# Graph kernel, start of the program: edge lists loaded by ScalarE's queue, x first on SyncE's, and eight transposes of x moved in place of idle ones

## The chip, the cores and the metric

The kernel runs on one core of a Trainium2 chip, in one launch. The metric is the device time of one execution in microseconds (us). A difference is told against runs of the kernel before.

## The reference, cut to what matters

Inputs are x (1024 nodes x 512 features), 32768 edges as two int32 lists `src` and `dst` (sorted by dst), and the weights of four layers. Each layer is a graph operation with a residual and a layer norm behind it:

```
edge_index = jnp.stack([src, dst])
x = _layernorm(x + L0(x, edge_index, w0, b0))   # D^-1/2 (A or A^T, plus I) D^-1/2 @ (x @ w0) + b0
x = _layernorm(x + L1(x, edge_index, ...))      # three graph convolutions, degrees by segment_sum over dst
x = _layernorm(x + L2(x, edge_index, ...))      # attention over the edges' mask
x = _layernorm(x + L3(x, edge_index, ...))      # relu(conv), conv
```

All layers need the same 1024 x 1024 matrix of edge counts. L0 also needs x @ w0.

## The kernel before, in words

Every engine has its own program, written out by hand in the order in which it runs; semaphores join them. No planner is used. What follows is the start, up to the end of the histogram loop, and what the change touches.

**Loads.** SyncE (SP) issues the DMAs one after the other (lines 382 to 396): dst and src into `edge_rows` (64 partitions x 512 each, 128 KB each), the low half of x into `xs` (1 MB), four rows of w0 (256 KB each), the high half of x, wq and wk (1 MB each), small bias rows, w1. The edges' loads count up `edges_in`, the halves of x `x_in[0]` and `x_in[1]`.

**From edges to keys.** VectorE zeroes five blocks of `count` (L1168), waits for both edge lists, and takes the low 7 bits and the rest of src (`bits`, L1170 and L1171), then the smallest and largest dst of each group and span (`group_lim`), the relative dst (`key_rows`) and diagonal matrices of the limits (`group_dia`). ScalarE converts the bits (L1000, L1002). TensorE transposes the three rows of keys (L615, which waits for `act_rows_set` and `rows_set`), ScalarE copies the turned keys (`edge_key`, L1004), VectorE adds them up (`keyed`) and casts them (`lo16`, L1192). The limits reach all partitions by one product of ones with `group_dia` into bank 0 (L620, "the limits' product"), which VectorE copies to `group_row` (L1195) and reduces to the number of rounds. Then VectorE enters its loop with the conversion of the keys (`key16`, L1252).

**The histogram loop.** The edges form 64 groups of 512. For each, VectorE writes one-hots (`lo_near` L1207, `hot_key` L1213), ScalarE the other half of them (distances L986, `lo_far` L993), TensorE multiplies them into one of four slots of PSUM (L626), and VectorE adds the two spans at the group's place in `count` (L1229). Four slots let TensorE run ahead of VectorE by that much. VectorE makes the one-hots of three groups before its first add, and reads the places of four groups at a time into registers (`places_at`, L1221).

**Pieces.** Between the histogram's matmuls TensorE works off a list of other units, cut into four pieces each: transposes of x (L548), of wq, wk (L552) and w1, the products x @ w0 (L587) and products of weights (L560 and on). `ORDER` is the list; `pieces[g]` gives the pieces that go behind group g, shared out by fixed weights (`TURNED` = 200 for a transpose, 1024 for a piece of a product; `SHARE` = 1280 per group), and `pieces[-1]`, sized by `EARLY`, those that go ahead of the first group: pieces 0 to 21, which are 16 transposes of the low half of x (units 0 to 3), two pieces of x @ w0 and four transposes of the high half. Unit n of these writes bank 4 + n % 4; ScalarE copies each finished unit out of PSUM (`copy_unit`) in its own order, the first four behind the first two groups' distances.

**Idle turns.** `idle_turns(n)` issues n transposes of the identity into bank 7, which nothing reads (L603). There are 16 at the start, 6 ahead of the third row of keys, 8 ahead of the limits' product, and 4 ahead of the pieces.

**ScalarE's start.** Its program begins with a copy of one column of `ones` into `esum` (L998), which waits for `const_set`, then the conversions of the bits. Its one table load bears the line of that copy.

Of the kernel before, what the change touches and what calls it, by code (L numbers as in the profile page):

```python
# [40 lines left out]
BODY = 16  # L41
HALF = 4
ZEROED = 5


def gnn_kernel(nc, x, src, dst, w0, b0, w1, b1, w2, b2, w3, b3, wq, bq, wk, bk, wv, bv, v1, c1, v2, c2, out):
# [5 lines left out]
    GE = CPG * P  # L52
# [7 lines left out]
    with ExitStack() as ctx:  # L60
# [9 lines left out]
        def at(name, start, shape, dt):  # L70
            return nc.alloc_sbuf_tensor_at(name, shape, dt, offset=start)
# [7 lines left out]
        def sem(name):  # L79
            return ctx.enter_context(nc.semaphore(name))  # L80
# [48 lines left out]
        edge_rows = at("edge_rows", r3 + 2 * W, [G, 2, GE], I32)  # L129
# [70 lines left out]
        edges_in = sem("edges_in")  # L200
# [71 lines left out]
        UNITS += [("bw", 0, 0)] + each("w12") + each("wf") + [("g", 0, 0)]  # L272
        NU = len(UNITS)
        upto = {kind: n + 1 for n, (kind, _, _) in enumerate(UNITS)}

        ORDER = []
        for n, (kind, _, _) in enumerate(UNITS):
            if kind in ("tb", "bw"):
                ORDER += [(m, k) for k in range(4) for m in (n, n + 1)]
            elif kind == "xw":  # L280
                turns = [(m, k) for m in (n - 2, n - 1) for k in range(4)]
                if n == 6:
                    ORDER += [(n, 0), (n, 1)] + turns[:6] + [(n, 2)] + turns[6:] + [(n, 3)]
                else:
                    for k in range(4):
                        ORDER += turns[2 * k:2 * k + 2] + [(n, k)]
            elif UNITS[n - 1][0] not in ("tb", "bw") and not any(u[0] == "xw" for u in UNITS[n + 1:n + 3]):
                ORDER += [(n, k) for k in range(4)]
# [6 lines left out]
        def ended(m):  # L295

            return sum(k == 3 for _, k in ORDER[:m])

        pieces = {}
        n, credit = 0, EARLY  # L300
        for g in range(-1, G - 1):
            m = n
# [73 lines left out]
        def wview(w):  # L376
            return w.rearrange("(c p) n -> p c n", p=P)

        @block.sync
        def _(sp):  # L380

            sp.dma_start(edge_rows[:, 0, :], dst.rearrange("(g e) -> g e", e=GE)).then_inc(edges_in, 16)
            sp.dma_start(edge_rows[:, 1, :], src.rearrange("(g e) -> g e", e=GE)).then_inc(edges_in, 16)
            for h in range(2):
                sp.dma_start(xs[:, HALF * h:HALF * (h + 1), :],
                             x[h * D:(h + 1) * D, :].rearrange("(b p) d -> p b d", p=P)).then_inc(x_in[h], 16)
                if h == 0:
                    for k in range(FB):
                        sp.dma_start(w0_sb[:, k, :], w0[k * P:(k + 1) * P, :]).then_inc(w0_in[k], 16)
            sp.dma_start(wq_sb[:], wview(wq)).then_inc(w_in["q"], 16)  # L390
            sp.dma_start(wk_sb[:], wview(wk)).then_inc(w_in["k"], 16)
            for n, b in enumerate((bq, bk, b1, b2)):
                sp.dma_start(brow[n * FB:(n + 1) * FB, :], b.rearrange("(c p) -> c p", p=P)).then_inc(cols_in, 16)
            for t, b in ((bias0, b0), (bias3, b3), (biasv, bv), (biasc1, c1)):
                sp.dma_start(t[:], b.partition_broadcast(P)).then_inc(rows_in, 16)
            sp.dma_start(w1_sb[:], wview(w1)).then_inc(w_in["1"], 16)
            sp.wait_ge(unit_done, upto["wqT"])
            sp.dma_start(w2_sb[:], wview(w2)).then_inc(w_in["2"], 16)
            sp.wait_ge(unit_done, upto["wkT"])
            sp.dma_start(w3_sb[:], wview(w3)).then_inc(w_in["3"], 16)  # L400
            sp.dma_start(wv_sb[:], wview(wv)).then_inc(w_in["v"], 16)
            sp.wait_ge(unit_out, NU)
            sp.dma_start(fold_rows[:, :], grow[:]).then_inc(fold_kept, 16)
            sp.wait_ge(fold_kept, 16)
            for n, t in enumerate((fold1, fold2)):
                sp.dma_start(t[:], fold_rows[n, :].partition_broadcast(P)).then_inc(fold_in, 16)
            sp.wait_ge(row_out, 1)
            sp.dma_start(degrees_kept[:], deg_row[0:1, :]).then_inc(deg_kept, 16)
            sp.wait_ge(deg_kept, 16)
            sp.dma_start(degs[:, 1, :], degrees_kept[0, :].rearrange("(j p) -> p j", p=P),  # L410
                         allow_slow_non_contiguous=True).then_inc(deg_in, 16)
            sp.wait_ge(part_done, len(PARTS))
            sp.dma_start(v1_sb[:], wview(v1)).then_inc(w_in["v1"], 16)
            sp.dma_start(v2_sb[:], wview(v2)).then_inc(w_in["v2"], 16)
            sp.dma_start(biasc2[:], c2.partition_broadcast(P)).then_inc(rows_in, 16)
            for j in range(NB - 1):
                sp.wait_ge(normed, 3 * NB + j + 1)
                sp.dma_start(out[j * P:(j + 1) * P, :], xs[:, j, :]).then_inc(stored, 16)
            for n, cols in enumerate((low_cols, high_cols)):
                sp.wait_ge(normed, 4 * NB + n)  # L420
                sp.dma_start(out[N - P:N, cols], xs[:, NB - 1, cols]).then_inc(stored, 16)
            sp.wait_ge(stored, 16 * (NB + 1))

        @block.gpsimd
        def _(pool):
# [23 lines left out]
            pool.wait_ge(rows_set, 2)  # L449
            nc.gpsimd.memset(count[:, ZEROED:NB, :].bitcast(F32), 0.0).then_inc(const_set, 1)  # L450
            pool.wait_ge(unit_out, upto["bT"])
# [81 lines left out]
        def _(pe):  # L533
# [66 lines left out]
            def idle_turns(count_):  # L600

                for n in range(count_):
                    pe.transpose(bank[:, HALF + 3, 0:P], ident[:], ident[:])  # L603
# [3 lines left out]
            for n in range(3):  # L607
# [7 lines left out]
                    mm = pe.transpose(bank[:, 2 + n // 2, at_col:at_col + G],  # L615
                                      key_rows[:, n, c * P:(c + 1) * P], ident[0:G, 0:G])
                mm.then_inc(rows_turned, 1)
            idle_turns(8)
            pe.wait_ge(rows_set, 2)
            pe.matmul(bank[:, 0, 0:2 * SPANS * G], ones[0:G, :], group_dia[:].rearrange("g a b -> g (a b)"),  # L620
                      start=True, stop=True).then_inc(rows_turned, 1)
# [5 lines left out]
                                 start=c % PAIR == 0, stop=c % PAIR == PAIR - 1)  # L627


            idle_turns(4)  # L630
            for m in range(*pieces[-1]):
                piece(m)
            for g in range(G):
                pe.wait_ge(win_added, max(2, g + 3 - SLOTS))
# [319 lines left out]
        def _(act):  # L954
# [39 lines left out]
                                     scale=-1.0, bias=ones[:, 0:1]).then_inc(act_hot_set, 1)  # L994


            act.wait_ge(const_set, 1)
            nc.scalar.copy(esum[:, 0, 0:1], ones[:, 0:1])  # L998
            act.wait_ge(bits_set, 1)
# [157 lines left out]
        def _(dve):  # L1157
# [3 lines left out]
            def then(ins):  # L1161

                chain[0] += 1
                ins.then_inc(dve_set, 1)
                dve.wait_ge(dve_set, chain[0])


            then(V.memset(count[:, 0:ZEROED, :].bitcast(F32), 0.0))  # L1168
            dve.wait_ge(edges_in, 32)
# [436 lines left out]
```

## Time and profile before

| | us |
|---|---|
| median of 3 runs | 567.65 (567.15 to 568.31) |
| the profiled execution's own time | 567.68 |
| its span, from the first to the last instruction | 565.9 |
| TensorE busy | 554.7 (98%) |
| VectorE busy | 332.0 (59%) |
| ScalarE busy | 169.5 (30%) |
| GpSimd busy | 128.2 (23%) |

The profiled execution's time is 1.8 us longer than its span, and times within the profile are counted from the span's start. Engines: PE is TensorE's matmuls, PEld its weight loads, DVE VectorE, ACT ScalarE, POOL GpSimd, SPq the issuing queue of SyncE; a name with q is an engine's sequencer. The granted clock of TensorE was at 90% or more of full speed in all 40 slices of the span.

### The profile page before, as it was taken

How to read it: one execution, taken by the hardware profiler on the slowest of the kernel's cores; microseconds unless marked ns; L12 is line 12 of the kernel's file. 1: busy time of each engine (PE TensorE's matmuls, PEld its weight loads, DVE VectorE, ACT ScalarE, POOL GpSimd, SP SyncE). 2: the span in 40 equal slices, each digit the busy share in tenths (PEclk: the TensorE clock that was granted, in tenths of full speed). 3: DMA queues.
4: the chain of work that ended last, by engine and by line, in shares of the span. 5: the costliest groups of instructions: out<-in, count | busy, mean ns of one | idle time of the engine just before them, and what ended most of it. 6: DMA issues, size and time to landing. Idle time of an engine off the chain costs nothing.

```text
span 565.9 us, 6587 instructions
## 1 busy us (share of the span) xinstructions
PE 554.7 (98%) x2179; PEld 346.5 (61%) x2179; DVE 332.0 (59%) x753; ACT 169.5 (30%) x364; POOL 128.2 (23%) x129
## 2 busy tenths in 40 slices
PE   8999999999999999999999999999999999999995
PEld 6655656445788744888865674544454686468643
DVE  7989898847687034225585984956374700540165
ACT  5998687455012222011040000321123103210200
POOL 3000000027234401203226630560410340000022
PEclk9999999999999999999999999999999999999999
DMA  8724000001000000000000000000040000000012
GB/s 291 250 76 148 2 1 1 2 0 38 1 3 1 0 1 0 0 1 0 2 3 0 1 0 0 1 1 0 1 167 0 2 0 1 0 0 1 0 57 95
DMA packets 9434, 16.24 MB, mean 29 GB/s; under 512 B 1571, under 2 KB 1843, under 8 KB 9398
## 3 DMA queue, kind: packets, MB, share of 16 engines
q1 hardware_dynamic: 9398, 15.75, 7.9%
q8 instruction: 24, 0.39, 0.3%
q14 instruction: 12, 0.10, 0.1%
HBM read 13.64 MB, written 2.11 MB: 28 GB/s over the span
## 4 chain that ended last, share of the span: by engine, by line
PE 90%; DVE 5%; issue 2%; DVEq 2%; ACT 0%; POOL 0%; POOLq 0%
PE bank L716 16%; PE bank L698 16%; PE bank L768 14%; PE bank L886 13%; PE bank L908 10%; PE bank L882 4%; PE bank L626 3%; PE bank L591 2%; PE bank L560 2%; PE bank L595 2%; DVE count L1229 2%; PE bank L587 2%; PE bank L898 1%; DVE hot_key L1213 1%; PE bank L603 1%
## 5 line engine op out<-in xcount | busy, mean ns | idle before, releaser
L472 POOL TENSOR_TENSOR rstd<-veps,mhalf 128x1 f32<-128x1 f32 x32 | 22.7, 710 | 207.8 <-DVE veps L1303 204.9
L908 PE MATMUL bank<-vv,probt 128*128 128x512 f32 x128 | 56.1, 592 | 0.0
L768 PE MATMUL bank<-v_sb,gt 128*128 128x512 f32 (+1 forms) x136 | 55.3, 567 | 0.0
L1229 DVE TENSOR_TENSOR count<-bank,count 128x192 f32 x128 | 45.7, 357 | 11.9 <-PE bank L626 7.9
L716 PE MATMUL bank<-adj,y_hi 128*128 128x512 f32 x128 | 51.5, 402 | 0.0
L716 PE MATMUL bank<-adj,y_lo 128*128 128x512 f32 x128 | 50.3, 393 | 0.0
L1310 DVE SCALAR_TENSOR_TENSOR xs<-bank,dinv,xs 128x512 f32<-128x512 f32 x23 | 17.0, 749 | 49.8 <-PE bank L768 37.3
L986 ACT ACTIVATE apart<-col_lo,edge_key 128x128 bf16<-128x128 int16 x128 | 44.2, 397 | 0.7 <-PE bank L615 0.7
L768 PEld LDWEIGHTS bank<-v_sb,gt 128*128 128x128 f32 x136 | 25.8, 190 | 28.8 <-issue 27.7
L908 PEld LDWEIGHTS bank<-vv,probt 128*128 128x128 f32 x128 | 23.9, 190 | 27.7 <-issue 27.7
L1213 DVE TENSOR_TENSOR hot_key<-col_key,key 128x384 bf16<-128x384 int16 x128 | 39.7, 351 | 0.1
L587 PE MATMUL bank<-w_sb,x0t 128*128 128x512 f32 x64 | 33.0, 599 | 0.3 <-ACT x0t L962 0.3
L993 ACT ACTIVATE lo_far<-apart,ones 128x256 bf16<-128x256 bf16 x64 | 32.2, 503 | 0.0
L626 PEld LDWEIGHTS bank<-hot_key,lo_near 128*128 128x128 bf16 x128 | 12.3, 100 | 31.9 <-issue 23.9
L505 POOL TENSOR_SCALAR mask<-count 128x1024 bf16<-128x1024 uint16 x8 | 23.1, 2894 | 37.6 <-DVE peak L1483 29.7
L1558 DVE SCALAR_TENSOR_TENSOR hidden<-bank,dinv,biasc 128x512 f32<-128x512 f32 x8 | 6.0, 751 | 37.6 <-PE bank L768 37.6
L716 PEld LDWEIGHTS bank<-adj,y_hi 128*128 128x128 f32 x128 | 24.1, 188 | 6.3 <-issue 0.5
L716 PEld LDWEIGHTS bank<-adj,y_lo 128*128 128x128 f32 x128 | 24.1, 188 | 5.9 <-issue 0.5
L768 PE MATMUL bank<-wfold,gt 128*128 128x512 f32 x64 | 27.6, 592 | 0.0
L1406 DVE TENSOR_TENSOR score<-bank,score 128x512 f32<-128x512 f32 x28 | 18.8, 688 | 13.6 <-PE bank L886 13.6
L698 PE MATMUL bank<-ya_hi,adj 128*128 128x512 f32 x64 | 25.6, 401 | 0.0
L716 PE MATMUL bank<-adj,yb_hi 128*128 128x512 f32 x64 | 25.5, 398 | 0.0
(221 smaller groups left out, 1071.1 us busy)
## 6 DMA issues: line engine op xcount, KB each, us to landing
w_sb<-in_L_gnn_W_dram SPq DMA_DIRECT2D x3, 1024.0 KB, 5.6
xs<-in_x_dram SPq DMA_DIRECT2D x2, 1024.0 KB, 7.3
v_sb<-in_L_gnn_W_dram SPq DMA_DIRECT2D x2, 1024.0 KB, 6.8
out_dram<-xs SPq DMA_DIRECT2D x7, 256.0 KB, 2.0
w_sb<-in_L_gnn_weight_dram SPq DMA_DIRECT2D x4, 256.0 KB, 6.4
wq_sb<-in_L_gnn_Wq_dram SPq DMA_DIRECT2D x1, 1024.0 KB, 10.5
wk_sb<-in_L_gnn_Wk_dram SPq DMA_DIRECT2D x1, 1024.0 KB, 12.8
wv_sb<-in_L_gnn_Wv_dram SPq DMA_DIRECT2D x1, 1024.0 KB, 7.8
```

Source lines behind the costliest of these rows:

```text
L505: then(nc.gpsimd.tensor_scalar(mask[:, m % 2, :], count[:, TILES[m], 0:N], 1.0, None, ALU.min))
L587: mm = pe.matmul(to, x0t[:, k, rows], w0_sb[:, k, :], start=first, stop=last)
L626: return pe.matmul(bank[:, slot, span], lo, hot_key[:, slot, c // PAIR, :, c % PAIR], start=c % PAIR == 0, stop=c % PAIR == PAIR - 1)
L698: mm = pe.matmul(to, m[:, k, j * P:(j + 1) * P], y[part][:, k, :], start=k == 0 and part == 0 and m is mat, stop=k == NB - 1 and part == 1 ...
L716: mm = pe.matmul(to, y[part][:, k, f * P:(f + 1) * P], m[:, k, half], start=n == 0 and part == 0 and m is mat, stop=n == NB - 1 and part = ...
L768: mm = pe.matmul(bank[:, 0 if cols is high_cols else HALF * (s % 2) + b, cols], g(k, j), w[:, k, cols], start=k == 0, stop=k == FB - 1)
L886: mm = pe.matmul(to, a[:, k, n * P:(n + 1) * P], b[:, k, :], start=k == 0, stop=k == 1)
L908: mm = pe.matmul(bank[:, 6 + m % 2, :], probt[:, m % 2, j, :], vv[:, j, :], start=j == 0, stop=j == NB - 1)
L986: ins = nc.scalar.activation(apart[:, n, c - BY_DVE, :], col_lo[:], ACT.Abs, scale=-1.0, bias=edge_key[:, 0, bass.ds(g + c * G, 1)])
L993: nc.scalar.activation(lo_far[:, slot], apart[:, n], ACT.Relu, scale=-1.0, bias=ones[:, 0:1]).then_inc(act_hot_set, 1)
L1213: V.tensor_tensor(hot_key[:, slot, n], col_key[:], key16[:, bass.ds(g, 1), n * PAIR:(n + 1) * PAIR].to_broadcast([P, KEYS, PAIR]), ALU.is_ ...
L1229: return V.tensor_tensor(count[:, :, bass.ds(at_dst, WIN)], bank[:, slot, n * KEYS:(n + 1) * KEYS].rearrange("p (h d) -> p h d", h=NB), co ...
```

## The change

The two edge loads leave SyncE's program and stand at the start of ScalarE's, dst first, ahead of the copy to `esum`. SyncE's first DMA is the low half of x. On TensorE the 8 idle turns ahead of the limits' product are replaced by the first 8 pieces (`OPENED` = 8: units 0 and 1, transposes of the low half of x); the 4 idle turns behind the product go, and the list goes on with piece 8. `pieces` itself, and so what follows each group, is unchanged.

```
+OPENED = 8
...
         @block.sync
         def _(sp):
 
-            sp.dma_start(edge_rows[:, 0, :], dst.rearrange("(g e) -> g e", e=GE)).then_inc(edges_in, 16)
-            sp.dma_start(edge_rows[:, 1, :], src.rearrange("(g e) -> g e", e=GE)).then_inc(edges_in, 16)
             for h in range(2):
                 sp.dma_start(xs[:, HALF * h:HALF * (h + 1), :],
...
                 mm.then_inc(rows_turned, 1)
-            idle_turns(8)
+            for m in range(OPENED):
+                piece(m)
             pe.wait_ge(rows_set, 2)
             pe.matmul(bank[:, 0, 0:2 * SPANS * G], ones[0:G, :], group_dia[:].rearrange("g a b -> g (a b)"),
                       start=True, stop=True).then_inc(rows_turned, 1)
...
-            idle_turns(4)
-            for m in range(*pieces[-1]):
+            for m in range(OPENED, pieces[-1][1]):
                 piece(m)
...
+            nc.scalar.dma_start(edge_rows[:, 0, :], dst.rearrange("(g e) -> g e", e=GE)).then_inc(edges_in, 16)
+            nc.scalar.dma_start(edge_rows[:, 1, :], src.rearrange("(g e) -> g e", e=GE)).then_inc(edges_in, 16)
             act.wait_ge(const_set, 1)
             nc.scalar.copy(esum[:, 0, 0:1], ones[:, 0:1])
```

## Rows read from the trace of the kernel before

**Rows 1.** The page: the chain that ended last, shares of the span by engine.
```profile
PE 90%; DVE 5%; issue 2%; DVEq 2%; ACT 0%; POOL 0%; POOLq 0%
```
**Rows 2.** Waits in 12 to 47 us: us in total, times, longest us.
```profile
PEld bank L626 <- DVE count L1229: 4.0, 6, 1.4
...
PE bank L626 <- DVE hot_key L1213: 1.5, 3, 0.9
```
**Rows 3.** Stretches: us, busy us (x instructions) by engine, PEclk, DMA share, GB/s.
```profile
24.00:47.00 23.00, 21.50 (x122) 12.23 (x119) 20.07 (x77) 21.99 (x63) 0.20 (x1) 1.00 0.15 53
47.00:60.00 13.00, 13.00 (x68) 7.49 (x67) 11.84 (x46) 10.48 (x30) 0.00 (x0) 1.00 0.46 161
```
**Rows 4.** The chain within 12.2 to 46.8 us, shares by line.
```profile
by line: DVE count L1229 28.3%; issue 20.8%; DVE hot_key L1213 18.7%; DVEq L1221 12.4%; DVE lo_near L1207 8.4%; DVEq L1229 2.9%; DVEq L1207 2.8%; DVEq L1213 1.7%; DVE key L1252 1.5%; DVE base_at L1254 0.8%; DVEq L1236 0.6%; DVE shift L1255 
```
**Rows 5.** The chain within 0 to 50 us in order: start us, us, what.
```profile
12.19 0.53 DVE key L1252
...
46.35 0.36 DVE hot_key L1213
...
46.84 0.52 PE bank L626 x4
```
**Rows 6.** The timeline from 0: start us, us, engine line op out<-in xcount [idle before].
```profile
0.72 1.28 ACT L998 ACT_TABLE_LOAD   x1 [0.72 <-PEq L1597]
...
0.72 0.55 SPq L382 DMA_DIRECT2D edge_rows<-in_dst_dram  x1
...
1.33 0.57 SPq L383 DMA_DIRECT2D edge_rows<-in_src_dram  x1
1.34 2.24 DVE L1168 MEMSET count<- 128x2620 f32 x1 [1.20 <-PEq L1597]
...
1.96 0.58 SPq L385 DMA_DIRECT2D xs<-in_x_dram  x1
2.01 0.19 ACT L998 COPY esum<-ones 128x1 f32<-128x1 f32 x1
...
2.02 3.67 PE L603 MATMUL bank<-ident 128*128 128x128 f32 x16 [2.02 <-POOL ones L438]
...
4.45 0.42 DVE L1170 TENSOR_SCALAR bits<-edge_rows 64x512 int32<-64x512 int32 x1 [0.87 <-DMA edge_rows<-in_src_dram]
...
7.70 1.09 PE L603 MATMUL bank<-ident 128*128 128x128 f32 x8
...
8.21 1.22 DVE L1192 CAST lo<-edge_key 128x128 int16<-128x128 f32 x1
...
8.73 0.70 PE L620 MATMUL bank<-group_dia,ones 64*128 64x256 f32 x2
...
9.85 1.91 PE L548 MATMUL bank<-ident,xs 128*128 128x128 f32 x16
...
10.48 2.06 ACT L962 COPY x0t<-bank 128x512 f32<-128x512 f32 x4 [1.30 <-PE bank L548]
...
13.45 0.62 DVE L1213 TENSOR_TENSOR hot_key<-col_key,key 128x384 bf16<-128x384 int16 x2
...
14.36 0.34 PE L626 MATMUL bank<-hot_key,lo_near 128*128 128x192 bf16 x2
```
**Rows 7.** DMA issues in 1.9 to 2.0 us: KB each, us from issue to landing.
```profile
xs<-in_x_dram SPq DMA_DIRECT2D x1, 1024.0 KB, 6.2
edge_rows<-in_src_dram SPq DMA_DIRECT2D x1, 128.0 KB, 3.0
```
**Rows 8.** Stretches of 0.5 us, columns as in rows 3.
```profile
3.50:4.00 0.50, 0.50 (x5) 0.50 (x4) 0.08 (x1) 0.00 (x0) 0.50 (x1) 1.00 1.46 102
4.00:4.50 0.50, 0.50 (x4) 0.50 (x4) 0.05 (x1) 0.00 (x0) 0.20 (x3) 1.00 0.09 25
4.50:5.00 0.50, 0.50 (x4) 0.50 (x3) 0.50 (x2) 0.10 (x1) 0.00 (x0) 1.00 0.86 336
...
7.50:8.00 0.50, 0.50 (x7) 0.43 (x7) 0.50 (x4) 0.10 (x1) 0.07 (x1) 1.00 1.05 402
```

More of the change, by code:

```diff
@@ L43 @@
 ZEROED = 5
+OPENED = 8
 def gnn_kernel(nc, x, src, dst, w0, b0, w1, b1, w2, b2, w3, b3, wq, bq, wk, bk, wv, bv, v1, c1, v2, c2, out):
@@ L380, in _ @@
         def _(sp):
-            sp.dma_start(edge_rows[:, 0, :], dst.rearrange("(g e) -> g e", e=GE)).then_inc(edges_in, 16)
-            sp.dma_start(edge_rows[:, 1, :], src.rearrange("(g e) -> g e", e=GE)).then_inc(edges_in, 16)
             for h in range(2):
@@ L617, in _ @@
                 mm.then_inc(rows_turned, 1)
-            idle_turns(8)
+            for m in range(OPENED):
+                piece(m)
             pe.wait_ge(rows_set, 2)
@@ L627, in chunk @@
                                  start=c % PAIR == 0, stop=c % PAIR == PAIR - 1)
-            idle_turns(4)
-            for m in range(*pieces[-1]):
+            for m in range(OPENED, pieces[-1][1]):
                 piece(m)
@@ L994, in far_one_hots @@
                                      scale=-1.0, bias=ones[:, 0:1]).then_inc(act_hot_set, 1)
+            nc.scalar.dma_start(edge_rows[:, 0, :], dst.rearrange("(g e) -> g e", e=GE)).then_inc(edges_in, 16)
+            nc.scalar.dma_start(edge_rows[:, 1, :], src.rearrange("(g e) -> g e", e=GE)).then_inc(edges_in, 16)
             act.wait_ge(const_set, 1)
```

## The prediction

> **What bounds the kernel now.** I read the chain of waits on the page first, then what TensorE waited for, then busy time by stretch, and last the start in order of time. The chain [rows 1] is 90% TensorE: over the span as a whole, work taken off its queue is worth its price, and so is an earlier start of it. The change only touches the first 15 us, so the question is which engine sets the time there. From 12 to 47 us it isn't TensorE. In the histogram loop TensorE stands still for VectorE, 4.0 us for the adds into `count` and 1.5 us for the key one-hots [rows 2], and is busy 21.5 of 23 us between 24 and 47 us, while after 47 us it is never idle [rows 3]. The chain from 12.2 to 46.8 us [rows 4] has only VectorE, its queue and issue time in its large shares; it runs from the key conversion at 12.19 us to the one-hots at 46.35 us, and TensorE takes it over only at 46.84 us [rows 5]. (`count` is also said to wait for TensorE there, but the chain puts these places down to VectorE's own register loads, L1221.) So up to 46.8 us the end moves with the moment at which VectorE starts, and a TensorE that is early waits longer.
>
> VectorE's start hangs on the edges. dst and src are issued at 0.72 and 1.33 us; src lands 3.0 us after its issue, 4.33 us, and VectorE begins at 4.45 us [rows 6, 7]. Its zeroing of `count` ended at 1.34 + 2.24 = 3.58 us, so it waited 0.87 us for data. From 4.45 to 12.19 us it runs nearly without a break on what it has; the one place where TensorE stands close is the limits' product: it begins at 8.73 us and takes 0.70 us, ends at 9.43 us, and VectorE's cast ahead of the copy that reads it ends at 8.21 + 1.22 = 9.43 us too [rows 6].
>
> **Part 1: twelve idle turns go, eight transposes of x come ahead of the product.** Removed are 8 turns (1.09 us) and the 4 behind the product. The 16 early transposes took 1.91 us, 0.12 us each, so eight are 0.96 us in the place of 1.09 us [rows 6]: the product comes at 8.73 us or up to 0.13 us sooner. Sooner is worth nothing, since the cast ends at 9.43 us anyhow. Behind the product 8 fewer transposes (0.96 us) and 4 fewer idle turns (at 1.09/8 each, 0.55 us) remain: TensorE is 1.5 us ahead. ScalarE's four copies of x, now from 10.48 us, come forward with them, and so do the first products with w0, and the first histogram matmul, at 14.36 us now, waits for the one-hots of VectorE (first pair 13.45 to 14.07 us) [rows 6]. It gains at most 0.5 us, and VectorE takes up that result no sooner, as it makes the one-hots of three groups first. From there the head start lies in TensorE's wait, which grows from the 5.5 us of [rows 2]. The split of the pieces over the groups doesn't change (the constants that share them out are the same), so no work moves from behind 46.8 us to the stretch where TensorE is idle. Value of part 1: 0. Bounds: 0 from the chain, and 1.5 us of gain if all of it came through.
>
> The cover: these transposes need the low half of x at 7.70 us. It was issued at 1.96 us and landed 6.2 us later, 8.16 us [rows 6, 7]; now issued at 0.72 us, and by the same 6.2 us, it lands at 6.9 us, 0.8 us in time. The edges' 256 KB between its packets cost at most 0.26 MB / 336 GB/s = 0.8 us more [rows 8]. Each us later than 7.70 would delay the product and with it VectorE one for one.
>
> **Part 2: SP issues x at once.** Two issues of 0.55 and 0.57 us with their gaps leave SP's queue, so all its DMAs come 1.96 - 0.72 = 1.24 us sooner [rows 6]: both halves of x, w0, and everything behind. All of them feed TensorE's pieces in the loop, which the chain doesn't run through; value 0. The high half, too, is not later than before, and its reader is in the covered stretch.
>
> **Part 3: ScalarE issues the edges.** No queued work of ScalarE is late: its next need is the conversion behind VectorE's bits, later than 4.45 us. If its two issues cost what SP's did, dst goes out at 0.72 us and src at 1.33 us, as before. The table load of 1.28 us [rows 6] would then run from about 1.9 to 3.2 us, beside the flight of the edges. What changes is company: x's 1 MB goes out with dst instead of behind src. The trace shows what x brings. From its issue at 1.96 us it took until about 4.5 us for the DMA engines to move data at full rate; in 3.5 to 4.0 us they were more than fully busy at 102 GB/s, in 4.0 to 4.5 us 25 GB/s passed, then 336 [rows 8]. Moved by 1.24 us, that slow stretch falls on 2.3 to 3.3 us, when the edges' bytes pass now. From 3.3 us the rest passes at 336 GB/s or more, shared with x: for src alone 2 x 0.131 MB / 336 GB/s = 0.8 us, for both twice that, 1.6 us. Last bytes at 4.1 to 4.9 us, and I add 0.3 us to the semaphore (an estimate): landing at 4.4 to 5.2 us, 0.1 to 0.9 us later than 4.33. I take 0.3 us later, near the lower end, as dst is out as early as x and part of it will slip through. Bounds: earlier by 0.4 us (below); later until all of x is in, 6.9 + 0.8 = 7.7 us, 3.4 us.
>
> The Trainium skill (DMA: Bandwidth & Descriptors, section Queues, rings and completion order) says that each DMA engine takes turns between queues by whole packets, 9 to 17 descriptors typically, and that a completion is written only after every earlier write of that engine, across its queues. It speaks against this change. The rows show each load on one queue alone and can't confirm it; the sum by it is the second rival below.
>
> **Sum.** 0 + 0 + 0.3 us. The profiled execution took 567.68 us at a span of 565.9 us, and the median of the runs is 567.65 us, the same. Forecast: 567.95 us, which is no change: the three runs spread over 1.2 us, and a difference under 0.2% (1.1 us) can't be told.
>
> **Rivals.**
> 1. Slower: the table load stays ahead of the DMA issues. It began at 0.72 us, the instant at which ScalarE's block starts, though the copy whose line it bears waited until 2.01 us [rows 6]. Both a load at the head of the block and one right ahead of that copy fit. If it is at the head, dst goes out at 2.0 us and src at 2.6 us, 1.28 us late, and with x already flowing I add 0.2 us: 569.1 us. It decides as soon as the load is the first instruction. The Trainium skill (ScalarE: Activation LUTs, section Step-by-step: what each stage is for) says that the load is placed right before the activation that needs it. By that rule this rival falls. Chance 0.15.
> 2. The edges queue behind runs of x's packets, as DMA engines take turns by runs of descriptors. A run in front of src of a third to a half of x's 2.7 us or more (1.05 MB at 402 GB/s [rows 8]) costs 0.9 to 1.4 us, the bound being 3.4 us: 568.8 us, and over 569 us in its tail. For it: the DMA engines were more than fully busy once x came. Against: only 64 rows of each edge list are to go in. Chance 0.09.
> 3. The edges come sooner, on a queue of their own. VectorE could start at 3.58 instead of 4.45 us. But TensorE's first 16 idle turns end at 5.69 us [rows 6], and the row transposes stand behind them; they now end nearly as the rows come. That leaves about 0.4 us: 567.25 us. Chance 0.11.
> 4. TensorE's 1.5 us comes through after all (the chain as inferred hides a wait for its chunks): 566.2 us. For it: ScalarE and VectorE are both nearly full in 24 to 47 us, and their order could be freed by it [rows 3]. Against: [rows 2, 5]. Chance 0.05.
>
> The clock: a new pause of about 1 us may come ahead of the first histogram matmul; pauses of up to 1.4 us [rows 2] left the granted clock at 1.00 in these stretches [rows 3], so I price it at nothing.
>
> **Chances and range.** Forecast 0.60. Faster by over 0.2% (below 566.5): rival 4 and a little noise, 0.06. Slower by over 0.2% (above 568.8): rival 1 most of the time, half of rival 2 and a tail of the forecast (src over 1.1 us late), 0.20. Within: 0.74. The range is 567.0 to 569.3 us: below it lie rival 4 and the lucky side of rival 3, above it the long waits of rival 2.
>
> **What would show it.** In the changed kernel's profile: ScalarE's first DMA issue at 0.7 us with the table load behind it (rival 1: at 2.0 us); VectorE's `bits` at 4.5 to 5.2 us; the product's start no more than 4.3 us behind `bits`, as now; transposes of x from 7.7 to 8.0 us without a wait for the DMA; the first `key` conversion 7.7 us behind `bits`; TensorE's wait for VectorE in 12 to 47 us larger by 1 to 1.5 us; and the 46.84 us moved by what `bits` moved. The forecast is wrong if `bits` moves by over 1 us, or if the end moves by something other than `bits` did.

## The result, and the profile after

The changed kernel takes 573.51 us (median; 573.21 to 574.10, 5 runs) against 567.65 us, a ratio of 1.0097 with a 95% interval of 1.0077 to 1.0116: 5.9 us slower. Its profiled execution took 573.51 us at a span of 571.7 us.

The timeline of the changed kernel from its start; the columns are those of rows 6, and ACTq is ScalarE's issuing queue.

```profile
0.72 0.44 SPq L384 DMA_DIRECT2D xs<-in_x_dram  x1
0.72 0.56 ACTq L996 DMA_DIRECT2D edge_rows<-in_dst_dram  x1
...
1.32 0.61 ACTq L997 DMA_DIRECT2D edge_rows<-in_src_dram  x1
...
1.96 1.28 ACT L999 ACT_TABLE_LOAD   x1 [1.96 <-issue]
...
2.02 3.28 PE L602 MATMUL bank<-ident 128*128 128x128 f32 x16 [2.02 <-POOL ones L437]
...
7.77 0.42 DVE L1171 TENSOR_SCALAR bits<-edge_rows 64x512 int32<-64x512 int32 x1 [4.19 <-DMA edge_rows<-in_src_dram]
...
8.90 1.22 PE L614 MATMUL bank<-ident,key_rows 64*128 64x64 f32 x8 [3.60 <-ACT key_rows L1001]
...
12.14 1.97 PE L547 MATMUL bank<-ident,xs 128*128 128x128 f32 x8
...
12.30 0.42 DVE L1192 TENSOR_TENSOR keyed<-bank,edge_key 128x256 f32<-128x256 f32 x1 [1.10 <-issue]
...
14.04 1.22 PE L620 MATMUL bank<-group_dia,ones 64*128 64x256 f32 x2
...
15.36 0.42 DVE L1196 COPY group_row<-bank 128x256 f32<-128x256 f32 x1 [2.49 <-PE bank L620]
```

The issues are where they were forecast, the table load stands behind them, and x isn't waited for. But `bits` starts at 7.77 us instead of 4.45 us [rows 6]. TensorE stands still for 3.60 us, and what it does behind that takes about twice as long: eight transposes take 1.97 us, where eight idle turns took 1.09 us, and the product 1.22 us instead of 0.70 us.

The DMA issues of the changed kernel (us from issue to landing):

```profile
edge_rows<-in_dst_dram ACTq DMA_DIRECT2D x1, 128.0 KB, 5.2
edge_rows<-in_src_dram ACTq DMA_DIRECT2D x1, 128.0 KB, 6.4
```

src took 3.0 us before [rows 7]; now 6.4. The changed kernel's chain within 0 to 60 us in order, columns as in rows 5:

```profile
1.32 6.35 DMA edge_rows<-in_src_dram
7.77 0.43 DVE bits L1171
...
18.03 0.53 DVE key L1253
...
52.68 0.53 PE bank L626 x4
```

From the key conversion to the place where TensorE takes over (called the handover below) it is 34.65 us, to the hundredth what it was (46.84 - 12.19 in [rows 5]). From there to the end of the span it is 519.0 us, and was 519.1. So all 5.84 us by which the handover is late were lost ahead of the key conversion: 7.77 - 4.45 = 3.32 us for the edges, and 10.26 - 7.74 = 2.52 us between `bits` and the key conversion. These two shares are those of one execution: in the profiles of this kernel and of its four variants below that change TensorE's program only (the queues alone, 44 and 54 turns, the product first) `bits` stood at 7.77 to 8.83 us.

What TensorE's clock did, in stretches of 1 us (columns of rows 3):

```profile
8.00:9.00 1.00, 0.10 (x1) 0.10 (x2) 1.00 (x3) 0.77 (x2) 0.00 (x0) 0.58 1.05 373
9.00:10.00 1.00, 1.00 (x8) 0.90 (x8) 0.96 (x3) 0.38 (x1) 0.00 (x0) 0.50 1.05 373
...
17.00:18.00 1.00, 1.00 (x3) 0.48 (x3) 0.00 (x0) 0.81 (x2) 0.00 (x0) 0.50 1.04 365
18.00:19.00 1.00, 1.00 (x3) 0.52 (x2) 0.91 (x3) 1.00 (x4) 0.00 (x0) 0.80 1.05 387
19.00:20.00 1.00, 1.00 (x7) 0.65 (x6) 0.96 (x5) 1.00 (x4) 0.00 (x0) 1.00 1.07 391
```

The granted clock falls to 0.50 (1.2 instead of 2.4 GHz) at the end of the pause and comes back past 18 us.

The 2.52 us can be read from VectorE. Two rows of the kernel before that weren't shown:

```profile
7.87 0.42 DVE L1191 TENSOR_TENSOR keyed<-bank,edge_key 128x256 f32<-128x256 f32 x1
...
9.53 0.42 DVE L1195 COPY group_row<-bank 128x256 f32<-128x256 f32 x1
```

From `bits` to `keyed` it was 3.42 us and is 4.53 us (1.11 more, for the third row of keys, which stands behind six slow idle turns); from `keyed` to `group_row` it was 1.66 us and is 3.06 us (1.40 more, for the eight transposes and the product). From `group_row` to the key conversion nothing differs (2.66 and 2.67 us).

### The profile page after: what moved, and what is told of

Read it like the earlier page. It is cut to its first block, busy times and chain, and to the rows that moved or that the text cites. A ratio compares the mean times of both kernels' runs of the same rounds, so it can differ in the third digit from the quotient of the medians.

```text
span 571.7 us, 6563 instructions
## 1 busy us (share of the span) xinstructions
PE 557.1 (97%) x2167; PEld 347.9 (61%) x2167; DVE 331.0 (58%) x753; ACT 169.8 (30%) x364; POOL 128.2 (22%) x129
## 4 chain that ended last, share of the span: by engine, by line
PE 89%; DVE 5%; issue 2%; DVEq 1%; DMA 1%; ACT 0%; POOL 0%; POOLq 0%; ACTq 0%
PE bank L715 16%; PE bank L697 16%; PE bank L767 14%; PE bank L885 13%; PE bank L907 10%; PE bank L881 4%; PE bank L626 3%; PE bank L590 2%; PE bank L559 2%; PE bank L594 2%; DVE count L1230 2%; PE bank L586 2%; PE bank L897 1%; DVE hot_key L1214 1%; DMA edge_rows<-in_src_dram 1%
## 5 line engine op out<-in xcount | busy, mean ns | idle before, releaser
L1230 DVE TENSOR_TENSOR count<-bank,count 128x192 f32 x128 | 45.7, 357 | 11.9 <-PE bank L626 6.6
L626 PEld LDWEIGHTS bank<-hot_key,lo_near 128*128 128x128 bf16 x128 | 12.2, 100 | 32.2 <-issue 21.9
```

Source lines behind the costliest of these rows:

```text
L626: return pe.matmul(bank[:, slot, span], lo, hot_key[:, slot, c // PAIR, :, c % PAIR], start=c % PAIR == 0, stop=c % PAIR == PAIR - 1)
L1230: return V.tensor_tensor(count[:, :, bass.ds(at_dst, WIN)], bank[:, slot, n * KEYS:(n + 1) * KEYS].rearrange("p (h d) -> p h d", h=NB), co ...
```

## Experiments

**Each half of the change alone.** Part 1 alone is the kernel before with these lines:

```
-            idle_turns(8)
+            for m in range(8):
+                piece(m)
...
-            idle_turns(4)
-            for m in range(*pieces[-1]):
+            for m in range(8, pieces[-1][1]):
```

> Part 1 alone: eight transposes of x in the place of the idle turns, all loads on SyncE as before. Theory (VectorE's path sets the end up to 47 us, and the loss came from the edges' loads and from TensorE's clock): x lands at 8.16 us as in the kernel before, the first transpose waits for it from 7.7 us, so the limits' product and with it VectorE come about 0.5 us later: 568.1 us. Rival A (TensorE's head start of 1.5 us comes through): 566.2 us. Rival B (the transposes ahead of the product are what cost): well over 570 us.

567.95 us (12 runs) against 567.71, ratio 1.0006 (0.9998 to 1.0015). Its chain:

```profile
12.34 0.52 DVE key L1252
...
46.98 0.52 PE bank L627 x4
```

The transposes waited 0.21 us for x, the product started at 8.87 us instead of 8.73, the key conversion came 0.15 us late, and so did the handover. TensorE's wait for VectorE in 12 to 47 us grew from 5.5 us to 8.1 us:

```profile
PEld bank L627 <- DVE count L1229: 6.4, 11, 1.4
PE bank L627 <- DVE hot_key L1213: 1.7, 3, 0.9
```

Its head start was lost there. Rivals A and B fall.

Parts 2 and 3 alone move the two edge loads to ScalarE and leave the idle turns.

> Parts 2 and 3 alone: the edges on ScalarE's queue, x first on SyncE's, idle turns as before. Theory: the edges land at about 7.7 us, TensorE's clock falls to the lower level as in the changed kernel, and 8 idle turns at that level cost as much ahead of the product as 8 transposes: 573.5 us. Rival B (the transposes are what cost): about 571 us (before plus 3.3 us).

573.88 us (5 runs), ratio 1.0111 (1.0097 to 1.0126): the whole loss comes with the loads. From its timeline:

```profile
8.83 0.42 DVE L1170 TENSOR_SCALAR bits<-edge_rows 64x512 int32<-64x512 int32 x1 [5.24 <-DMA edge_rows<-in_src_dram]
...
13.19 1.86 PE L601 MATMUL bank<-ident 128*128 128x128 f32 x8
```

Eight idle turns take 1.86 us instead of 1.09, though the granted clock is recorded as 1.00 in every stretch of this execution: the durations show the low speed where the record of the clock doesn't. In both forms (0.50 recorded, or not) the times are alike. In this execution the edges were 4.38 us late and the key conversion, at 18.46 us, lost another 1.89 us behind them.

**Why the edges were late.** First the queue without company:

```
+            sp.wait_ge(edges_in, 32)
             for h in range(2):
                 sp.dma_start(xs[:, ...
```

> The edges on ScalarE's queue, but SyncE waits for both of them before it issues x; idle turns as before. Theory (the edges were late because x and w0 went out beside them): ScalarE's two loads land as SyncE's did, src at about 4.3 us, bits at 4.45 us. Rival (ScalarE's queue is slower in itself, or the table load behind the issues holds it up): src still lands at 6 us or later. The time isn't the test here: x lands at about 10.5 us, 2.3 us later than before, which delays the first pieces; 567.7 to 570 us.

```profile
4.08 0.42 DVE L1171 TENSOR_SCALAR bits<-edge_rows 64x512 int32<-64x512 int32 x1 [0.50 <-DMA edge_rows<-in_src_dram]
```

ScalarE's queue alone is as quick as SyncE's, even with the table load behind the issues: in the five profiles in which SyncE loads both lists ahead of x, `bits` stood at 4.02 to 4.45 us. The time was 568.44 us (ratio 1.0014, 1.0005 to 1.0022), as x's high half is waited for.

Then the size of x's DMAs, in the changed kernel:

```
-                sp.dma_start(xs[:, HALF * h:HALF * (h + 1), :], ...).then_inc(x_in[h], 16)
+                for b in range(HALF * h, HALF * (h + 1)):
+                    sp.dma_start(xs[:, b, :], x[b * P:(b + 1) * P, :]).then_inc(x_in[h], 16)
...
-                    pe.wait_ge(x_in[h], 16)
+                    pe.wait_ge(x_in[h], 16 * HALF)
```

> The changed kernel with each half of x loaded by four DMAs of 256 KB instead of one of 1 MB; the bytes, the rows of 2 KB and the queues are the same. Theory (a load of the other queue is let in only once the descriptors of the load ahead of it are through, so that dst waited for the whole of x and src for w0 as well): dst starts behind the first quarter, src behind the second or third, and bits starts at 5.0 to 5.5 us instead of 7.77; TensorE hardly pauses; 568.3 to 568.8 us. Rival (the edges only share bandwidth with x and w0 row by row): bits stays at 7.7 to 8.8 us and the time at 573.5 us.

571.03 us (568.47 to 572.11, 6 runs), ratio 1.0054 (1.0037 to 1.0071), `bits` at 6.49 us: between the two, and later than I had expected. The queues tell more. Per queue (q1 is SyncE's, q10 ScalarE's): packets, MB and share of the engines, in the changed kernel from 0 to 4.0 us

```profile
q1 hardware_dynamic: 264, 0.54, 44.8%
```

and, again from 0, to 5.7 us:

```profile
q1 hardware_dynamic: 493, 1.01, 56.5%
q10 hardware_dynamic: 80, 0.13, 6.1%
```

A packet is one row of 2 KB here. x's low half has 512 of them and each edge list 64, and at the end of a DMA come 16 short writes. The trace doesn't say which of the 16 DMA engines moved a row; rows per engine are counts divided by 16 here: 32 for x's low half, 4 for an edge list. At 4.0 us the engines have run 264 rows of x, 16.5 each, and none of dst, which was issued beside x. (With x behind the edges, 36 of dst's rows were through at 2.5 us.) At 5.7 us all of dst is through (64 rows and 16 writes) and nothing of src, behind 493 rows, 31 each. With x in four DMAs of 8 rows for each engine, to 3.0, to 3.5 and to 4.0 us:

```profile
q1 hardware_dynamic: 132, 0.25, 25.0%
q10 hardware_dynamic: 14, 0.03, 5.0%
```
```profile
q1 hardware_dynamic: 179, 0.33, 27.6%
q10 hardware_dynamic: 80, 0.13, 12.1%
```
```profile
q1 hardware_dynamic: 257, 0.49, 36.9%
q10 hardware_dynamic: 83, 0.14, 14.2%
```

dst comes in behind some 8 rows of x per engine and is through at 3.5 us; src's first rows follow at 4.0 us, behind some 16. So the engines change from one queue to the other by runs: 16 rows of x, dst, 16 rows of x, src; or 8, dst, 8, src. Why src then took until 6.4 us to land stays open; its packets ran from 4.0 to 6.0 us, and 245 of SyncE's queue passed beside them.

With two DMAs for each half of x, 16 rows each:

> The changed kernel with each half of x loaded by two DMAs of 512 KB, 16 rows of 2 KB per DMA engine each. Theory (the engines change queues behind runs of at most 16 rows, so that dst stands behind the first half of x's 32 rows per engine and src behind the second half): nothing changes against the changed kernel; dst starts at about 4.0 us behind some 260 rows of x, src near 6 us, bits at 7.8 to 8.8 us, 573 to 574 us. Rival (the other queue gets in at the end of each DMA, whatever its size): in the changed kernel dst would have stood behind all of x, and here dst and src would come in one after the other half, so bits at 7.8 us too, but then dst's rows start in the changed kernel only behind 512 of x's, which its count of 264 at 4.0 us speaks against; a third way, that the count of DMAs in flight matters, would give bits at 6.5 to 7.1 us, between the quarters and the changed kernel.

572.68 us (6 runs), ratio 1.0082 (1.0067 to 1.0096), `bits` at 7.34 us. To 3.5 us:

```profile
q1 hardware_dynamic: 244, 0.49, 40.9%
q10 hardware_dynamic: 3, 0.01, 0.5%
```

dst again stands behind 15 rows per engine, though it comes 0.5 us sooner, as x's first rows did. That is nearer to the changed kernel than to the quarters, but `bits` is sooner than the 7.8 us at least that I had expected.

> The changed kernel, but SyncE waits for both edge lists behind its load of x's low half; w0 and all else come behind. Theory: dst starts at about 4.1 us as in the changed kernel, src right behind it instead of at 6 us, bits at about 5.4 us, 568.6 to 569.5 us. Rival (x alone holds up both loads, w0 has no part): bits at 7.7 us or later and 573.5 us.

```
             if h == 0:
+                sp.wait_ge(edges_in, 32)
                 for k in range(FB):
```

572.93 us (4 runs), ratio 1.0090 (1.0075 to 1.0104), `bits` at 7.83 us. My theory was wrong: w0 has no part. The second run of 16 rows, behind which src stands, is x's too.

**What TensorE's pause costs.** In the kernel before, `idle_turns(16)` becomes `idle_turns(2)`:

> The kernel before with 2 idle turns at its start in place of 16; the loads are as before. It measures TensorE's pause by itself: it stands still from about 2.5 to 5.6 us, about as long as in the changed kernel, with the edges on time. Theory (behind such a pause its instructions take twice as long for 5 us and more): bits at 4.4 us, 8 idle turns ahead of the product take about 1.9 instead of 1.09 us, the key conversion comes about 1.9 us later, at 14.1 us, 569.5 us. Rival (the pause is free, the rest of the loss has another cause): 567.7 us.

571.23 us (568.99 to 571.49, 5 runs), ratio 1.0063 (1.0050 to 1.0076). The edges are on time and TensorE is slow:

```profile
4.02 0.46 DVE L1170 TENSOR_SCALAR bits<-edge_rows 64x512 int32<-64x512 int32 x1 [0.43 <-DMA edge_rows<-in_src_dram]
...
8.42 1.77 PE L603 MATMUL bank<-ident 128*128 128x128 f32 x8
...
13.59 0.51 DVE L1252 TENSOR_SCALAR key<-keyed,shift 128x256 int16<-128x256 f32 x1 [1.11 <-issue]
```

In the profiled execution the pause alone costs 1.4 us at the key conversion (1.8 us behind `bits`, which was 0.4 us sooner here); four of the five runs lie 2.3 us above that execution. The same kernel once more:

> The same kernel as the one with 2 idle turns, once more: its profiled execution (568.99 us) was 2.3 us shorter than its other four (571.21 to 571.49), with key conversion 1.4 us late. Theory (two forms of the slow stretch): the times fall near 569 and near 571.3 us again; a profile near 571.3 us shows a longer slow stretch, the key conversion 3.5 us late. Rival (the additional 2.3 us is lost elsewhere, behind the loop): the key conversion 1.4 us late again, and the rest behind 110 us.

571.20 us (569.12 to 571.64, 6 runs): two groups again, and the profiled execution is once more the short one (the key conversion at 13.77 us). A long one wasn't profiled here; the split with 13 turns (below) shows one, with the key conversion 10.3 us behind `bits` instead of 9.6, and the product and the first pieces slow as well.

The other way round, the changed kernel with its pause filled by idle turns, 44 and then 54 in place of 16:

> The changed kernel with 44 idle turns at the start in place of 16, so that TensorE works until the keys come. Theory (3.3 us from the edges, 2.5 us from the clock): the granted clock stays at 1.00, the key conversion starts at 15.5 us and the end comes 3.3 us after that of before: 571.0 us. Rival (the whole 5.9 us comes from the edges and what hangs on them, the clock's fall is hidden): 573.5 us.

> The changed kernel with 54 idle turns at the start, which end at about 9.9 us, behind the keys, so that TensorE has no pause at all. Theory (the pause is what makes its instructions slow, at a granted clock of 1.00 or of 0.50): the eight transposes ahead of the product take 1.1 us instead of 2.0, the key conversion comes 7.7 to 8.5 us behind bits instead of 10.3, the end at 571 to 572.5 us with the edges at 7.8 to 8.5 us. Rival (the late edges or x and w0 in flight bring the slow stretch, the pause doesn't): transposes at 2.0 us, 573.5 us or more.

574.26 us (4 runs; 1.0110, 1.0095 to 1.0125) and 574.46 us (5 runs; 1.0115, 1.0099 to 1.0131). As times both miss. With 44 turns, 1.16 us of pause was left and the granted clock fell at 11.9 us all the same. With 54 there was none, and TensorE kept its speed:

```profile
12.64 1.09 PE L547 MATMUL bank<-ident,xs 128*128 128x128 f32 x8
...
13.66 0.70 PE L620 MATMUL bank<-group_dia,ones 64*128 64x256 f32 x2
...
17.14 0.52 DVE L1253 TENSOR_SCALAR key<-keyed,shift 128x256 int16<-128x256 f32 x1 [1.11 <-issue]
```

`bits` was at 8.59 us there, and the key conversion 8.55 us behind it, of which 1.1 us are turns too many. So in the changed kernel it is the pause that makes TensorE slow, not the late edges or the transfers, which were the same here. As a time the gain isn't shown, for both kernels have a new stand of TensorE near 289 us (1.62 and 2.76 us in the profiled executions), which no other kernel shows and whose cause stays open. With 54 turns the granted clock was at 0.50 again behind it (292 to 294 us), and from the handover to the end it was 523.1 us instead of 519.0.

**How near the edge the turns are.**

> A version meant to beat both: the kernel before, with dst alone issued by ScalarE, src by SyncE, both at 0.72 us, x behind src, and 13 idle turns at the start in place of 16, so that they end with the keys. Theory: no row of x stands ahead of an edge row on either queue; both lists land at 3.4 to 3.9 us, bits at 3.65 to 4.0 us, the key conversion 0.5 to 0.8 us sooner than before (11.4 to 11.7 us), 566.8 to 567.2 us. Rival (ScalarE's queue comes second wherever x is in flight, and x is issued 0.6 us sooner here): dst lands at 5 us or later, 568 us or more.

```
-            sp.dma_start(edge_rows[:, 0, :], dst...)
...
+            nc.scalar.dma_start(edge_rows[:, 0, :], dst...)
...
-            idle_turns(16)
+            idle_turns(13)
```

569.81 us (567.05 to 571.57, 12 runs). The edges came as expected, `bits` at 3.89 us, but in the profiled execution (570.63 us) eight idle turns took 1.97 us, though TensorE had hardly paused ahead of the keys (13 turns from 2.02 to 5.06 us):

```profile
5.10 1.22 PE L614 MATMUL bank<-ident,key_rows 64*128 64x64 f32 x8
...
8.33 1.97 PE L602 MATMUL bank<-ident 128*128 128x128 f32 x8
```

Four of the runs lie at 567.05 to 567.5 us, eight at 568.9 to 571.6 us. Split or turns?

> The kernel before with 13 idle turns in place of 16 at the start, loads as before. Theory (how much TensorE does before the keys decides when it gets fast): part of the runs near 567.5 us, part at 569 to 571.5 us, as in the version with the split. Rival (three turns don't matter; the split does): all runs within 567.2 to 568.3 us.

568.52 us (12 runs): six at 567.2 to 567.9, six at 569.1 to 571.4 us. It is the turns. In its profiled execution, one of the short ones, 13 turns took 3.04 us, as in the long one with the split, and eight took 1.09 us. The kernel before, run beside it, had 3 of 23 executions at 569.6 to 571.3 us; it may be that even 16 turns don't always do, but none of these executions was profiled.

> The kernel before with dst alone issued by ScalarE, src and x behind it by SyncE, and all 16 idle turns kept. Theory (the split brings the edges 0.5 us sooner, and the 13 turns of the version before this one were what kept TensorE slow in its longer runs): bits at 3.9 us, the key conversion at 11.7 to 12.0 us, all runs within 567.0 to 567.6 us, none near 571. Rival (the split itself, not the turns, brings the slow runs): times spread up to 571 us again.

567.54 us (567.26 to 568.15, 12 runs) against 567.93 us, ratio 0.9987 (0.9975 to 0.9999), with no long execution:

```profile
12.02 0.53 DVE key L1252
...
46.69 0.53 PE bank L625 x4
```

`bits` at 4.07 us, the key conversion 0.17 us sooner, the handover 0.15 us. This has the lowest median here, but a gain isn't shown. The interval ends just under one, and part of it are the three long executions of the kernel beside it; `bits` at 4.07 us lies within the 4.02 to 4.45 us that the profiles with the old loads have; and none long of 12 is no clear difference from 3 of 23.

**The order at the product.** In the changed kernel the limits' product goes ahead of the eight transposes:

> The changed kernel with the limits' product ahead of the eight transposes. Theory (at the lower speed the transposes stand in VectorE's way, which waited 2.5 us for the product): the product starts about 4.4 us behind bits instead of 6.3 us, the key conversion comes 1.2 to 1.5 us sooner relative to bits, 572.0 to 572.3 us where the edges land as in the changed kernel. Rival (the order is free): 573.5 us.

572.61 us (4 runs), ratio 1.0089 (1.0075 to 1.0104). `bits` was at 8.42 us and the key conversion at 16.58 us, 8.16 us behind it instead of 10.26: 2.1 us back, more than I had expected. The pieces, all behind the product now and slow, took part of that again: the handover is 35.23 us behind the key conversion instead of 34.65.

## Why the prediction was wrong

- **What bounds the start** was right, closely: in 13 of the 16 profiled executions the handover came 34.62 to 34.67 us behind the key conversion, whatever came before. It was later in the three where the first pieces were late: 35.5 us with x behind the edges, 35.2 with the product first, 35.7 in the long execution of the split with 13 turns.
- **Part 1** at 0 was right: 0.2 us of median, 0.15 us in the profile. Its bound of 1.5 us was not touched.
- **Part 3** failed, by how the engines are shared. I let x and the edges share them row by row, and took +0.3 us from a range of 0.1 to 0.9. What came was +3.32 us, at the far bound of 3.4 us. The step at fault is "dst is out as early as x and part of it will slip through". Rival 2 named the mechanism, but with one run of a third to a half of x ahead of src; there are two of about half of x, one ahead of each list, and its chance of 0.09 was too small. (Its 2.7 us for x is 1.05 MB / 402 GB/s = 2.6 us.) The Trainium skill (DMA: Bandwidth & Descriptors, section Queues, rings and completion order) says that an engine drains a whole packet, 9 to 17 descriptors typically, before it changes queues; the counts agree, with some 16 rows per engine, or 8 where a DMA has no more.
- **The clock**, priced "at nothing", was the second fault: with it "the first `key` conversion 7.7 us behind `bits`" failed, which came 10.26 us behind, 2.52 us more. I looked for a pause in front of the loop, and didn't ask what late edges do to TensorE: its 16 turns end at 5.3 us, and each us that the keys come later is a us of stand. TensorE was slow behind pauses of 1.16 us (44 turns) and 1.92 us (x in quarters) and fast behind one of 0.26 us (13 turns, the profiled execution); where between them the loss begins no run shows, but edges a us or more late had to be priced with it. The pauses of [rows 2], up to 1.4 us in the loop, left the clock at 1.00 and didn't carry over to the start.
- **Rival 1** is excluded by the row: the table load began at 1.96 us, behind the issues. The Trainium skill (ScalarE: Activation LUTs, section Step-by-step: what each stage is for) says that the load is placed right before the activation that needs it; the trace agrees. **Rival 3** did not come, as x was beside the edges on the other queue; with dst alone on ScalarE's queue the key conversion was 0.17 us sooner instead of 0.4, which is within the scatter of `bits`. **Rival 4** falls with part 1 alone.

## What to carry to other kernels

A short load that everything waits for must not be issued beside a long one on another queue: here it wasn't served in proportion but behind a run of the other's rows, once for each of the two edge lists. Put it first in time; cutting the long one into smaller DMAs gave back part. When a load may come late, price also what the engines that wait do with the time, above all whether TensorE keeps working, and look at the durations of like instructions, not at the recorded clock alone. Time saved on an engine that waits for another in the next stage is worth nothing until that wait is gone.

## What the runs showed of the hardware

- The two hardware queues were served in turn by runs of about 16 rows of 2 KB per DMA engine (264 rows of x on 16 engines ahead of dst's first), and of 8 where a DMA had 8.
- TensorE's first turns take 0.23 us each on average (16 in 3.67 us), later ones 0.14 us. With 13 turns instead of 16, six of 12 executions took 569.1 to 571.4 us, the others 567.2 to 567.9 us.
- A pause of 1.16 us behind 44 turns was followed by a granted clock of 0.50 from 11.9 us to past 18 us, one of 0.26 us behind 13 turns by eight turns in 1.09 us.
- VectorE's cast to `lo16` took 1.22 us in the kernel before, where GpSimd zeroes its part of `count` at the same time (7.93 to 9.34 us), and 0.23 us in the changed one, where it began at 12.64 us and that zeroing ended at 12.66. It hid behind the product there.
